# Four transformer layers in one program on one core: the opening in another order, and new slots in the plan of the attention items

## The chip, the cores and the metric

The kernel runs on one core of a Trainium2 chip, in one launch. What is measured is the device time in microseconds, the median over several executions. Lower is better.

## What is computed

The input is x, 4 batches of 512 rows of 128 features, with a context of 4 x 154 x 128 and masks over its 154 keys. Four layers follow one another. Each adds an attention over the context to x and then a feed-forward part:

```python
x = x + _L0_xattn_ref(_layernorm(x), ctx, ctx, mask_ik0, ...)   # 16 heads of 8, 64 memory keys and values beside the context's
x = x + _L0_ffn_ref(_layernorm(x), W1, b1, W2, b2, scale)        # gelu, low-rank terms taken from rows of the normalized x
x = x + _L1_xattn_ref(_layernorm(x), ctx, ...)                   # queries and keys scaled by their root mean square
x = x + _L1_ffn_ref(_layernorm(x), ...)                          # router, 4 experts of 512, silu
x = x + _L2_xattn_ref(_layernorm(x), ctx, ctx, mask_bf1, ...)    # rotary queries and keys
x = x + _L2_ffn_ref(_layernorm(x), ...)                          # router, 8 experts of 352 and a shared one of 176
x = x + _L3_xattn_ref(_layernorm(x), ctx, ctx, ...)              # one head of 128
x = x + _L3_ffn_ref(_layernorm(x), ...)                          # gate, two projections
```

## The kernel before

The work is cut into items: one part of one layer for one batch. Layers 0, 1 and 2 have four attention items each, numbered a = 0 to 11 here; the feed-forward items of layer 0 have no place of their own but are spread over the attention items 1 to 5, and the others (F1, F2, A3, F3) follow their layer's attention. Each engine runs its own instruction stream, written out by hand, and the streams meet at semaphores: an engine does its instructions strictly in the order of the code, and one that waits holds all behind it.

An attention item has 28 slots (layer 0, 7 chunks of keys by 4 groups of heads) or 20, and a tail of 3 or 4. In slot n TensorE computes one block of scores (`attention_step`, L1000, into bank 0 or 1), ScalarE its exponent (`exps`, L1773), and TensorE, some slots later, the products with the values (L1021) and with a mask for the denominators (L1031). The exponent's argument has the row's maximum already subtracted: the negated maxima are fed to the score matmul as rows of the queries' tile, and the head that each column belongs to is picked by constant rows of the keys' tile. So the item before must have prepared, for item a:

- keys: projection (`kproj`: `k_proj` L782, `k_bias` L1233), their square, mean square and Newton steps in layer 1 (`k1` to `k3`: L1890, L1239, L579 to L585), split in a high part and a low part (`ksplit` L1638 on ScalarE, `klow` L1930 on GpSimd), transposes (`kt`, L796), and copies into the keys' tile, one per head and masked, by ScalarE (`kb`, L1648) and VectorE (L1269);
- queries: the same on x (`xt` L843 and L1668, `q` L854 and L1289, `q1` to `q4`, `qsplit` L1690, `qlow` L1937), transposed per group (`qxt`, L865, copied at L1696);
- maxima: 32 score blocks over all keys for two heads each (`max`: `scores_for_max` L880), reduced by VectorE (`maxima`, L1327), transposed in two parts (`mt`, L890, L1703) and put into the queries' tile by DMAs (L629);
- values: `v`, L818, L820 and L1257.

The constant rows of the keys' tile, 5 partitions (96 to 100) of all columns, are written once per tile by `shift_rows` (L594) from the small table `maskk`: two tiles of layer 0 (`arena`, 3488 columns each) and two of the later layers (`kb_sb`, 2464 each). The 64 memory keys of layer 0 go into columns of both `arena` tiles (L1833, 4 heads each), after GpSimd scaled and split them (L2023 to L2030) and TensorE transposed them (L1171); the memory values are rows built at L2033.

Which slot of an item carries which piece is said by a table: a row of `SLOTS` serves two attention items (a // 2), a row of `SLOTS0` one batch of layer 0's feed-forward, whose slot numbers run on from attention item b + 1 into the next. `attention_plan` turns them into lists of pieces per slot, and each engine's loop takes the pieces that it has a part in. The pieces of a slot follow that slot's score block, exponent or values. `rden` are the reciprocals of the denominators (L1281, VectorE), `vs` the copy of the values (L1783, ScalarE), `on` their product (L1960, GpSimd), `finish` the output projection (L1043), `ln` and `norm` a layer norm (L1223, L1867 to L1884), `w` a chunk of feed-forward weights (DMA L645, ScalarE L1710, GpSimd L1966). `TAIL` is the number of slots that an item takes beyond its score blocks.

What precedes item 0 is the opening: constants and loads, then the preparation above for items 0 and 1, written out in each engine's code. PSUM has 8 banks; in the opening all are shared, in an attention item four (2 to 5) serve the preparation. `take_bank` picks the one taken longest ago, and TensorE waits until its last reader is done.

## Time and profile before

| | |
|---|---|
| median of 3 runs | 1012.13 us (1011.17 to 1013.39) |
| the profiled execution, own time | 1012.16 us |
| its span | 1010.4 us |
| TensorE's mean granted clock | 0.955 |
| busy: TensorE, VectorE, ScalarE, GpSimd | 912.1, 581.9, 432.4, 283.9 us |
| first score block of items 0, 1, 6, 8 | 58.55, 98.55, 332.28, 566.84 us |

PE is TensorE, DVE VectorE, ACT ScalarE, POOL GpSimd and SP the engine that issues the DMAs. The times of a timeline are microseconds from the span's start; the bracket tells how long the engine had been idle and what ended that. A releaser is inferred: of several semaphores it is the one that came last. The granted clock is 1.00 at 2.4 GHz and 0.50 at 1.2 GHz; a matmul is then twice as long. An fp32 matmul of this kernel counts as several instructions, so a group of 4 can be x8.

### The profile page before, as it was taken

What the parts mean: (1) busy time and instruction counts of PE and PEld (TensorE: products, weight loads), DVE (VectorE), ACT (ScalarE), POOL (GpSimd) and SP (SyncE); (2) the same over time, 40 slices, a digit from 0 to 9 for tenths busy, and PEclk for the clock granted to TensorE, in tenths of its full rate; (3) what the DMA queues carried; (4) which work ended last, traced back from release to release, by engine and by line L of the source; (5) the groups of instructions that cost most, each with busy time, mean ns of one, the idle gap of its engine ahead of it and who ended that gap; (6) DMA issues with size and microseconds to landing.
All of it is one profiled execution on the core that took longest, in us unless ns stands there. A gap on an engine that the chain in (4) does not pass through costs nothing. (4 is left out here: it accounts for less than half of the span.)

```text
span 1010.4 us, 15438 instructions
## 1 busy us (share of the span) xinstructions
PE 912.1 (90%) x5522; PEld 648.1 (64%) x5522; DVE 581.9 (58%) x1403; ACT 432.4 (43%) x795; POOL 283.9 (28%) x404
## 2 busy tenths in 40 slices
PE   2689999999999898999989799998999999999776
PEld 2555446465555444888877545545888878888665
DVE  3665757675757574455556367674536454354477
ACT  1345555667654555233332356655223232222330
POOL 7411514545644532010211055332001010010243
PEclk9989989999979799999999889999999999999995
DMA  6000000000010210000000211100000000000001
GB/s 153 4 2 14 1 15 2 15 2 18 19 53 2 76 36 9 14 1 1 1 1 1 77 29 37 44 24 13 2 1 1 1 1 1 1 1 1 1 1 42
DMA packets 27573, 18.10 MB, mean 18 GB/s; under 512 B 6221, under 2 KB 25770, under 8 KB 27370
## 3 DMA queue, kind: packets, MB, share of 16 engines
q1 hardware_dynamic: 27498, 17.12, 6.1%
q8 instruction: 45, 0.74, 0.3%
q14 instruction: 30, 0.25, 0.1%
HBM read 15.63 MB, written 1.05 MB: 17 GB/s over the span
## 5 line engine op out<-in xcount | busy, mean ns | idle before, releaser
L1327 DVE TENSOR_REDUCE mneg<-PS 128x2 f32<-128x308 f32 (+1 forms) x384 | 180.4, 515 | 115.5 <-PE PS L880 114.7
L1490 DVE TENSOR_TENSOR work<-PS,work 128x512 f32<-128x512 f32 (+2 forms) x168 | 114.8, 685 | 169.3 <-PE PS L1065 126.1
L1796 ACT ACTIVATE work<-PS 128x512 f32<-128x512 f32 (+2 forms) x168 | 99.8, 596 | 245.9 <-PE PS L1065 232.1
L1773 ACT ACTIVATE work<-PS 124x512 f32<-124x512 f32 (+1 forms) x272 | 156.8, 601 | 92.8 <-PE PS L1000 91.9
L1079 PEld LDWEIGHTS PS<-down_w,work 128*128 128x128 f32 (+2 forms) x1344 | 157.8, 191 | 5.7 <-DVE work L1490 1.3
L1079 PE MATMUL PS<-down_w,work 128*128 128x128 f32 (+2 forms) x1344 | 158.3, 275 | 1.0 <-DVE work L1490 1.0
L1063 PE MATMUL PS<-xh_sb,arena 128*128 128x512 f32 (+2 forms) x336 | 138.0, 411 | 9.6 <-DVE work L1490 9.6
L1065 PE MATMUL PS<-xh_sb,arena 128*128 128x512 f32 (+2 forms) x336 | 132.6, 395 | 0.0
L1064 PE MATMUL PS<-xl_sb,arena 128*128 128x512 f32 (+2 forms) x336 | 132.0, 393 | 0.0
L1867 POOL TENSOR_SCALAR rstd<-bn_mv 128x4 f32<-128x4 f32 x32 | 7.3, 227 | 436.2 <-DVE bn_mv L1225 436.1
L880 PEld LDWEIGHTS PS<-kb_sb,qxt_sb 97*128 97x128 f32 x256 | 45.4, 197 | 63.5 <-issue 33.8
L1000 PE MATMUL PS<-qxt_sb,kb_sb 101*124 101x512 f32 x160 | 71.3, 462 | 9.3 <-ACT work L1773 8.8
L1063 PEld LDWEIGHTS PS<-xh_sb,arena 128*128 128x128 f32 (+2 forms) x336 | 61.1, 182 | 28.8 <-DVE work L1490 14.3
L1021 PE MATMUL PS<-work,vb_sb 124*32 124x512 f32 (+1 forms) x544 | 78.2, 649 | 0.7 <-ACT work L1773 0.7
L880 PE MATMUL PS<-kb_sb,qxt_sb 97*128 97x308 f32 x256 | 71.7, 350 | 6.8 <-DVE mneg L1327 3.8
L1031 PE MATMUL PS<-work,mv_sb 124*32 124x512 f32 (+1 forms) x544 | 74.1, 618 | 0.0
L1065 PEld LDWEIGHTS PS<-xh_sb,arena 128*128 128x128 f32 (+2 forms) x336 | 60.9, 181 | 17.1
L1064 PEld LDWEIGHTS PS<-xl_sb,arena 128*128 128x128 f32 (+2 forms) x336 | 61.2, 182 | 12.6
L1518 DVE SCALAR_TENSOR_TENSOR x_res<-PS,gates_sb,x_res 128x128 f32<-128x128 f32 x192 | 53.5, 340 | 5.9 <-PE PS L1079 5.9
L1000 PE MATMUL PS<-qxt_sb,arena 101*125 101x512 f32 x112 | 50.8, 454 | 1.6 <-ACT work L1773 1.0
L880 PE MATMUL PS<-arena,qxt_sb 97*128 97x436 f32 x128 | 46.1, 416 | 6.0 <-DVE vb_sb L1257 2.8
L1000 PEld LDWEIGHTS PS<-qxt_sb,kb_sb 101*124 101x124 f32 x160 | 30.2, 195 | 29.9 <-ACT work L1773 21.9
(183 smaller groups left out, 1277.4 us busy)
## 6 DMA issues: line engine op xcount, KB each, us to landing
ctx_rep<-in_ctxT SPq DMA_DIRECT2D x12, 308.0 KB, 3.2
stage<-in_w SPq DMA_DIRECT2D x8, 256.0 KB, 4.2
stage<-in_wg SPq DMA_DIRECT2D x8, 176.0 KB, 2.4
stage<-in_wu SPq DMA_DIRECT2D x8, 176.0 KB, 2.4
x_res<-in_x SPq DMA_DIRECT2D x4, 256.0 KB, 3.9
down_w<-in_w SPq DMA_DIRECT2D x1, 1024.0 KB
...
```

What stands on the lines that cost most here:

```text
L880: pe.matmul(PS[:, bank, 0:w], QXT[0:KX_ROWS, a % 2, g, t * 128:(t + 1) * 128], KB(layer)[0:KX_ROWS, a % 2, g, f * w:(f + 1) * w], start=Tr ...
L1000: pe.matmul(PS[0:rows, n % 2, :], KB(layer)[0:K_ALL, a % 2, g, c * rows:(c + 1) * rows], QXT[0:K_ALL, a % 2, g, :], start=True, stop=True) ...
L1021: pe.matmul(PS[32 * g:32 * g + 32, 6, :], VB[0:rows, a % 2, c, g * 32:(g + 1) * 32], p_tile(i, 4 * c + g)[0:rows, :], start=(c == 0), stop ...
L1031: pe.matmul(PS[32 * g:32 * g + 32, 7, :], mask[0:rows, c, :], p_tile(i, 4 * c + g)[0:rows, :], start=(c == 0), stop=(c == chunks - 1)).the ...
L1063: pe.matmul(o, w[0], xH[:, i % 2, :], start=True, stop=False)
L1064: pe.matmul(o, w[0], xL[:, i % 2, :], start=False, stop=False)
L1065: pe.matmul(o, w[1], xH[:, i % 2, :], start=False, stop=True).then_inc(*sig["up"].mark((i, kt, m)))
L1079: mm = pe.matmul(PS[:, bank, t * 128:(t + 1) * 128], HH[0:rows, bank - 6, j, t * 128:(t + 1) * 128], rhs, start=(j == 0), stop=(j == len(t ...
L1327: dve.tensor_reduce(mneg[:, a % 2, t, h0:h0 + 2], PS[:, bank_of["mx", a, m], 0:2 * (KT0 if layer == 0 else KC)].rearrange("p (h n) -> p h ...
L1490: dve.tensor_tensor(HH[0:rows, e % 2, j, :], PS[0:rows, 2 * (n % 2) + 1, :], SS[0:rows, n % 2, :], ALU.mult).then_inc(*sig["h"].mark((i, n)))
L1773: act.activation(p_tile(i, n)[0:rows, :], PS[0:rows, n % 2, :], ACT.Exp, scale=SCALE).then_inc(*sig["p"].mark((i, n)))
L1796: act.activation(SS[0:rows, n % 2, :], PS[0:rows, bank, :], ACT.Silu).then_inc(*sig["act"].mark((i, n)))
```

## The change

1. `shift_rows` becomes an activation (Copy), and ScalarE does all four at the head of its stream, before the first x. The load of `maskk` goes to the head of SP's stream with a semaphore of its own.
2. VectorE: the masks' preparation comes ahead of item 0's key bias, the query bias ahead of the value bias; the layer norm sums of item 1 come ahead of `kb_out(0)`, and item 1's key and query biases stand after the 8th and the 14th maximum. The value masks move from after the 14th and 26th maximum to after the 20th and 26th.
3. TensorE: value bias after the queries' projection; the key transposes before those of the memory keys, which now wait for the memory keys alone (`"l"`) and not for the memory values; item 1's transposes and projections stand between the maxima. Bank 6 is held for the memory keys until the last of the opening's maxima.
4. ScalarE: the memory keys of item 0's tile are copied alone (4 operations), those of item 1's tile after its queries' split. `scores_for_max` waits for its own tile's.
5. GpSimd: item 0's low query part comes ahead of the memory keys, item 1's layer norm ahead of the memory values, and the two additions of the output bias to x are taken out of the layer norms and put behind item 1's low parts.
6. The table. Its rows for items 0 to 3 put `vs` and `rden` at slots 2 and 3 where there was 0 (item 0 has none). Queries, keys and weights move by one to four slots in all rows; of layer 0's feed-forward the last batch moves two slots forward, and all `ln` from 9 to 6. The tail of item 10 goes from 4 slots to 3.

```diff
-            eng.tensor_copy(KB(layer)[PR:K_ALL, r, :, 0:w].rearrange("p g (h n) -> p g h n", h=HL),
-                            maskk[PR:K_ALL, None, :, None].to_broadcast([K_ALL - PR, G, HL, w // HL])).then_inc(
+            eng.activation(KB(layer)[PR:K_ALL, r, :, 0:w].rearrange("p g (h n) -> p g h n", h=HL),
+                           maskk[PR:K_ALL, None, :, None].to_broadcast([K_ALL - PR, G, HL, w // HL]), ACT.Copy).then_inc(
...
+            load(maskk[:, :], A["maskk"], "maskk_in", 0)
             xv = A["x"].rearrange("b (t p) d -> p b t d", p=128)
...
                     if a < 2:
-                        pe.wait_ge(*sig["mem_kb"].at(0))
+                        pe.wait_ge(*sig["mem_kb"].at(a))
...
             k_proj(None, 0)
-            value_bias(None, 0)
             xt(None, 0)
             q_proj(None, 0)
-
-            pe.wait_ge(*sig["mem_ready"].at(0))
+            value_bias(None, 0)
+            k_transposes(None, 0)
+
+            pe.wait_ge(*sig["mem_ready"].at("l"))
...
-            k_transposes(None, 0)
-            xt(None, 1)
-            k_proj(None, 1)
             for g in range(G):
                 qxt(None, 0, g)
-            q_proj(None, 1)
             for m in range(N_MAX):
                 scores_for_max(None, 0, m)
-                if m == 8:
+                if m == 4:
+                    xt(None, 1)
+                    k_proj(None, 1)
+                if m == 10:
+                    q_proj(None, 1)
+                if m == 16:
                     v_blocks(None, 0, 0)
-                if m == 20:
+                if m == 22:
                     v_blocks(None, 0, 1)
...
+            act.wait_ge(*sig["maskk_in"].at(0))
+            for n in range(4):
+                shift_rows(act, n // 2, n % 2)
             xt_out(0)
...
-            layer_norm(0)
+            layer_norm(0, bias=False)
             k_finish(0)
             k_low(0)
+            q_low(0)
             pool.wait_ge(*sig["mem_in"].at(0))
...
+            layer_norm(1, bias=False)
             _, mem_cols = layout0(MR)
...
-            q_low(0)
-            layer_norm(1)
             k_finish(1)
             k_low(1)
             q_low(1)
-
-            pool.wait_ge(*sig["qx_l"].at(1))
-            for r_ in range(2):
-                shift_rows(pool, 1, r_)
-                pool.wait_ge(*sig["shift_rows"].at((True, r_)))
+            bias_into_x(0)
+            bias_into_x(1)
```

Of the table the row for items 8 and 9 stands here for all:

```diff
-    {"vs": 0, "rden": (0, 0, 0, 0), "on": 1, "finish": 6, "ln": (1, 2, 3, 4), "norm": 5, "kt": 0, "kb": (0, 0, 1, 1), "qxt": (2, 3, 5, 6),
-     "max": (5, 20), "mt": (1, 21), "v": (21, 20), "xt": 7, "q": 9, "q1": 11, "q2": 13, "q3": 14, "q4": 18, "qsplit": 19, "qlow": 20, "kproj": 13,
-     "k1": 10, "k2": 12, "k3": 14, "ksplit": 20, "klow": 21, "w": 4},
+    {"vs": 0, "rden": (0, 0, 0, 0), "on": 1, "finish": 6, "ln": (1, 2, 3, 4), "norm": 5, "kt": 0, "kb": (0, 0, 1, 1), "qxt": (3, 3, 5, 6),
+     "max": (5, 20), "mt": (1, 21), "v": (20, 21), "xt": 7, "q": 9, "q1": 11, "q2": 16, "q3": 16, "q4": 20, "qsplit": 21, "qlow": 22, "kproj": 12,
+     "k1": 10, "k2": 11, "k3": 14, "ksplit": 20, "klow": 21, "w": 7},
```

The order of ScalarE's instructions in the opening, before:

```order
L1668 ACT_TABLE_LOAD
L1668 ACTIVATE xt_sb<-PS 128x512
L1638 ACTIVATE kx_sb<-k_sb 77x8x4x8 x2
L1690 ACTIVATE qx_sb<-q_sb 128x16x4x8 x2
L1648 ACTIVATE arena<-PS,maskk_sb 97x2x154 x4
L1833 ACTIVATE arena<-PS,maskk_sb 97x4x64 x8
L1668 ACTIVATE xt_sb<-PS 128x512
L1696 ACTIVATE qxt_sb<-PS 97x512 x4
```

and with the change (its lines are numbered two higher there):

```order
L594 ACT_TABLE_LOAD
L594 ACTIVATE arena<-maskk_sb 5x4x872 x2
L594 ACTIVATE kb_sb<-maskk_sb 5x4x616 x2
L1670 ACTIVATE xt_sb<-PS 128x512
L1640 ACTIVATE kx_sb<-k_sb 77x8x4x8 x2
L1692 ACTIVATE qx_sb<-q_sb 128x16x4x8 x2
L1650 ACTIVATE arena<-PS,maskk_sb 97x2x154 x4
L1832 ACTIVATE arena<-PS,maskk_sb 97x4x64 x4
L1698 ACTIVATE qxt_sb<-PS 97x512 x4
```

The four constant rows stand ahead of all, half of the memory keys ahead of the query blocks, and item 1's x behind them. TensorE in the same place, before:

```order
L782 MATMUL PS<-w_attn,ctxT_sb 77x128 x2
L831 MATMUL PS<-w_attn,b_v 128x128
L843 MATMUL PS<-ident_sb,xn_sb 128x128 x4
L854 MATMUL PS<-w_attn,xt_sb 128x128 x4
L1171 MATMUL PS<-ident_sb,stage 97x64 x4
L796 MATMUL PS<-ident_sb,kx_sb 97x77 x8
L843 MATMUL PS<-ident_sb,xn_sb 128x128 x4
L782 MATMUL PS<-w_attn,ctxT_sb 77x128 x2
L865 MATMUL PS<-ident_sb,qx_sb 97x128 x16
L854 MATMUL PS<-w_attn,xt_sb 128x128 x4
L880 MATMUL PS<-arena,qxt_sb 128x436 x9
```

and with the change:

```order
L782 MATMUL PS<-w_attn,ctxT_sb 77x128 x2
L843 MATMUL PS<-ident_sb,xn_sb 128x128 x4
L854 MATMUL PS<-w_attn,xt_sb 128x128 x4
L831 MATMUL PS<-w_attn,b_v 128x128
L796 MATMUL PS<-ident_sb,kx_sb 97x77 x8
L1172 MATMUL PS<-ident_sb,stage 97x64 x4
L865 MATMUL PS<-ident_sb,qx_sb 97x128 x16
L880 MATMUL PS<-arena,qxt_sb 128x436 x5
L843 MATMUL PS<-ident_sb,xn_sb 128x128 x4
L782 MATMUL PS<-w_attn,ctxT_sb 77x128 x2
L880 MATMUL PS<-arena,qxt_sb 128x436 x6
L854 MATMUL PS<-w_attn,xt_sb 128x128 x4
```

Item 0's query blocks and first maxima no longer stand behind item 1's x. VectorE in item 5, where the queries and keys of item 7 are prepared (`mneg` are the maxima of item 6), before:

```order
L1327 TENSOR_REDUCE mneg<-PS 128x2 x15
L1289 TENSOR_TENSOR q_sb<-PS,b_q 128x512
L1233 TENSOR_TENSOR k_sb<-PS,b_k 77x256
L1327 TENSOR_REDUCE mneg<-PS 128x2 x4
L1239 TENSOR_REDUCE k_ms_sb<-ka_sb 77x32
L571 TENSOR_SCALAR k_ms_sb<-k_ms_sb 77x32
L573 TENSOR_SCALAR k_rr_sb<-k_ms_sb 77x32
L1327 TENSOR_REDUCE mneg<-PS 128x2 x2
L1297 TENSOR_REDUCE q_ms_sb<-qa_sb 128x64
L571 TENSOR_SCALAR q_ms_sb<-q_ms_sb 128x64
L573 TENSOR_SCALAR q_rr_sb<-q_ms_sb 128x64
L1327 TENSOR_REDUCE mneg<-PS 128x2 x8
```

and with the change:

```order
L1331 TENSOR_REDUCE mneg<-PS 128x2 x14
L1293 TENSOR_TENSOR q_sb<-PS,b_q 128x512
L1237 TENSOR_TENSOR k_sb<-PS,b_k 77x256
L1331 TENSOR_REDUCE mneg<-PS 128x2 x3
L1301 TENSOR_REDUCE q_ms_sb<-qa_sb 128x64
L571 TENSOR_SCALAR q_ms_sb<-q_ms_sb 128x64
L573 TENSOR_SCALAR q_rr_sb<-q_ms_sb 128x64
L1243 TENSOR_REDUCE k_ms_sb<-ka_sb 77x32
L571 TENSOR_SCALAR k_ms_sb<-k_ms_sb 77x32
L573 TENSOR_SCALAR k_rr_sb<-k_ms_sb 77x32
L1331 TENSOR_REDUCE mneg<-PS 128x2 x6
```

Two maxima come ahead of these rows in both. The queries' seed (L573, `q_rr_sb`) now comes first, after 19 of the item's 32 maxima instead of 23, and the keys' follows it.

## Rows read from the trace of the kernel before

**Rows 1.** The page: busy us (share of the span) xinstructions of each engine.

```profile
PE 912.1 (90%) x5522; PEld 648.1 (64%) x5522; DVE 581.9 (58%) x1403; ACT 432.4 (43%) x795; POOL 283.9 (28%) x404
```

**Rows 2.** Timeline, 10-24 us: start, us, engine, line, operation [idle before <-releaser].

```profile
11.93 0.60 ACT L1668 ACTIVATE xt_sb<-PS 128x512 f32<-128x512 f32 x1 [9.93 <-PE PS L843]
...
12.58 2.07 PE L854 MATMUL PS<-w_attn,xt_sb 128*128 128x128 f32 x8 [0.69 <-ACT xt_sb L1668]
...
13.33 4.28 DVE L594 CAST arena<-maskk_sb 5x3488 fp32r<-5x3488 f32 x2
...
13.45 2.33 POOL L1920 TENSOR_TENSOR k_sb<-k_sb,keep 77x256 f32<-77x256 f32 x1 [0.66 <-DVE kbias L1590]
...
17.64 0.69 DVE L1289 TENSOR_TENSOR q_sb<-PS,b_q 128x512 f32<-128x512 f32 x1
...
18.32 0.55 POOL L2023 TENSOR_SCALAR stage<-stage 64x128 f32<-64x128 f32 x1
...
18.37 1.15 ACT L1690 ACTIVATE qx_sb<-q_sb 128x512 fp32r<-128x512 f32 x2 [1.84 <-DVE q_sb L1289]
...
19.54 0.45 POOL L2030 TENSOR_TENSOR stage<-stage 64x128 f32<-64x128 f32 x1
...
22.46 0.91 PE L1171 MATMUL PS<-ident_sb,stage 64*97 64x64 f32 x4 [7.80 <-POOL down_w L2033]
...
22.48 1.26 POOL L1937 TENSOR_TENSOR qx_sb<-q_sb,qx_sb 128x512 f32<-128x512 f32 x1
```

**Rows 3.** The timeline, 24 to 59 us.

```profile
26.54 3.04 ACT L1833 ACTIVATE arena<-PS,maskk_sb 97x256 fp32r<-97x256 f32 x8
...
31.72 1.11 PE L843 MATMUL PS<-ident_sb,xn_sb 128*128 128x128 f32 x4 [6.83 <-POOL xn_sb L1874]
...
33.48 3.21 PE L865 MATMUL PS<-ident_sb,qx_sb 128*97 128x128 f32 x16
...
34.23 0.61 POOL L1920 TENSOR_TENSOR k_sb<-k_sb,keep 77x256 f32<-77x256 f32 x1 [1.15 <-DVE k_sb L1233]
...
37.34 2.07 PE L880 MATMUL PS<-arena,qxt_sb 97*128 97x436 f32 x9
...
53.76 3.23 DVE L1327 TENSOR_REDUCE mneg<-PS 128x2 f32<-128x436 f32 x6
...
58.55 0.79 PE L1000 MATMUL PS<-qxt_sb,arena 101*125 101x512 f32 x1 [0.49 <-DMA qxt_sb<-mt_sb]
```

**Rows 4.** Groups by form, ScalarE: busy us, mean ns | idle before.

```profile
L1796 ACT ACTIVATE work<-PS 128x512 f32<-128x512 f32 x128 | 76.1, 597 | 149.4 <-PE PS L1065 135.6 <-PE PS L1043 12.1 <-DVE work L1490 1.5
...
L1821 ACT ACTIVATE work<-PS 77x1024 f32<-77x1024 f32 x4 | 4.1, 1019 | 4.2 <-PE PS L1136 4.2
```

**Rows 5.** DMA issues of the first 60 us: KB, us to landing.

```profile
bqk_sb<-in_bk SPq DMA_DIRECT2D x1, 0.5 KB, 2.1
```

**Rows 6.** Timeline, end of item 5 and start of 6: GpSimd, then TensorE.

```profile
324.07 0.29 POOL L579 TENSOR_TENSOR q_tmp<-q_rr_sb 128x64 f32<-128x64 f32 x1 [3.34 <-DVE q_rr_sb L573]
...
335.63 0.72 POOL L1930 TENSOR_TENSOR kx_sb<-k_sb,kx_sb 77x256 f32<-77x256 f32 x1
...
336.41 1.53 PE L796 MATMUL PS<-ident_sb,kx_sb 77*97 77x77 f32 x8 [3.64 <-POOL kx_sb L1930]
```

**Rows 7.** The timeline in item 8: ScalarE, then TensorE.

```profile
579.65 0.50 ACT L1710 ACTIVATE arena<-stage 128x352 fp32r<-128x352 f32 x1 [4.89 <-DMA stage<-in_wg]
...
581.17 0.55 PE L880 MATMUL PS<-kb_sb,qxt_sb 97*128 97x308 f32 x2 [1.98 <-ACT qxt_sb L1696]
```

**Rows 8.** The timeline at the start of item 1: VectorE.

```profile
98.77 3.39 DVE L1281 RECIPROCAL work<-PS 128x128 f32<-128x128 f32 x4 [0.55 <-PE PS L1031]
```

**Rows 9.** Windows, L1000 alone: us, busy (instructions), PEclk, DMA share, GB/s.

```profile
336.50:346.80 10.30, 4.15 (x6) 1.75 (x6) 0.50 0.14 53
...
346.80:357.10 10.30, 3.18 (x8) 1.48 (x8) 1.00 0.01 2
...
582.30:589.10 6.80, 1.41 (x2) 0.65 (x2) 0.50 0.11 30
```

More of the change, by code:

```diff
@@ L673, in _ @@
                     load(mvT[:, :], A["mvT0"], "mem_in", 0)
-                    load(maskk[:, :], A["maskk"], "const_in", 0)
                     load(MV0[:, :, :], A["mv0"], "const_in", 0)
@@ L1821, in attention3_step, with memory_keys @@
                     act.activation(PT3, PS[0:KJ, 6:8, :], ACT.Copy).then_inc(*sig["a3_pt"].mark(i))
+            def memory_keys(r):
+                if r == 0:
+                    act.wait_ge(*sig["mem_kt_psum"].at(0))
+                act.wait_ge(*shift_signal(0).at((False, r)))
+                mem_cols = KB0[:, r, :, 0:HL * KT0].rearrange("p g (h n) -> p g h n", h=HL)[:, :, :, KC:KT0]
+                for h in range(HL):
+                    act.activation(mem_cols[0:KX_ROWS, :, h, :], PS[0:KX_ROWS, 6, 0:G * KM].rearrange("p (g n) -> p g n", g=G), ACT.Copy,
+                                   scale=maskk[0:KX_ROWS, h:h + 1]).then_inc(*sig["mem_kb"].more(r))
+            act.wait_ge(*sig["maskk_in"].at(0))
+            for n in range(4):
+                shift_rows(act, n // 2, n % 2)
             xt_out(0)
@@ L1827, in _ @@
                 kb_out(0, h)
-            act.wait_ge(*sig["mem_kt_psum"].at(0))
-            for r_ in range(2):
-                mem_cols = KB0[:, r_, :, 0:HL * KT0].rearrange("p g (h n) -> p g h n", h=HL)[:, :, :, KC:KT0]
-                for h in range(HL):
-                    act.activation(mem_cols[0:KX_ROWS, :, h, :], PS[0:KX_ROWS, 6, 0:G * KM].rearrange("p (g n) -> p g n", g=G), ACT.Copy,
-                                   scale=maskk[0:KX_ROWS, h:h + 1]).then_inc(*sig["mem_kb"].more(0))
-            xt_out(1)
+            memory_keys(0)
             for g in range(G):
                 qxt_out(None, 0, g)
+            xt_out(1)
             k_split(1)
             q_split(1)
+            memory_keys(1)
             mt_out(None, 0, 0)
@@ L1857, in _, with layer_norm @@
         def _(pool):
-            def layer_norm(j):
+            def layer_norm(j, bias=True):
                 b = ITEMS[j][2]
@@ L1875, in layer_norm, with bias_into_x @@
                                    ALU.mult).then_inc(*sig["xn"].mark(j))
-                slot = bias_slot(j)
+                if bias:
+                    bias_into_x(j)
+            def bias_into_x(j):
+                b, slot = ITEMS[j][2], bias_slot(j)
                 if slot is not None:
```

25 lines of the change are left out of this document (13 added, 12 removed), and 44 rows, old and new, of tables (SLOTS, SLOTS0).

## Prediction

> **What bounds the kernel now.** The page's busy shares come first: TensorE is busy for 90% of the span, VectorE 58%, ScalarE 43%, GpSimd 28% [rows 1]. So time is to be had only where TensorE is idle, or where its clock is at the half level; the page's clock line shows such slices in the opening, in the attention items and at the end. The timeline of the opening comes next, because there TensorE is busy for little of the time: the first exponent's score matmul starts at 58.55 us [rows 3]. Two chains fill that time. The first is GpSimd's: it works one thing after the other, and TensorE, in order, stands 7.80 us for the memory keys' and values' preparation, although the keys alone (L2023 to L2030, done at 19.99) are what its next transposes read [rows 2]. Then it waits 6.83 us for the second item's normalized x at 31.72, with the queries of item 0, whose low part GpSimd had finished at 23.74, queued behind it [rows 2, 3]. The second chain is VectorE's: 32 maxima that TensorE feeds from 37.34 and that end at 56.99, 0.53 us each (the last six took 3.23), with two value masks between them [rows 3]. The last view is the timeline at TensorE's stalls in the attention items, with the windows for the clock there.
>
> **The opening.** I follow the changed order along the chain.
>
> Constant rows. VectorE did two casts of 3488 columns in 4.28 us from 13.33 [rows 2], GpSimd two of 2464 after 40.9. All four go to ScalarE. No row has such an operation there; the nearest are 1024 columns in 1.019 us and 512 in 0.597 [rows 4], so 0.824 ns a column: 0.597 + 2976 x 0.824 ns = 3.05 us for 3488 columns and 2.21 us for 2464, 10.5 us for the four; neighbours overlap by a tenth of a microsecond, so 10.2. The Trainium skill speaks against the move (ScalarE: Activation LUTs, Rules for kernel authors: plain arithmetic belongs on VectorE, which is faster by the column). The rows agree on the column, 2.14 against 3.05 us, and by that rule alone the change would lose 0.9 us on each of the two large casts, 1014 us; rival 2 is its strong form. What decides is not the column's price, but that ScalarE has nothing to do until 11.93 [rows 2]. The selector table's load becomes SP's first: small loads land 2.1 us after issue [rows 5], so from 0.72 us, with a microsecond of doubt for the first of all, it is there at 2.8 to 3.8, and ScalarE is free at about 13.4. Every other load is issued 0.3 to 0.45 us later. The transposed x is copied from 13.5 where it would have been 12.2: **ScalarE's queue costs 1.3 us** here (0 if the columns ran as on VectorE, 4 if they were twice as dear).
>
> Queries of item 0. Copy until 14.1; the projection, 2.07 us at 1.2 GHz [rows 2], until 16.2; bias 0.69, no longer behind the casts, until 17.0; split 1.15: 18.2; GpSimd's low part 1.26: 19.5 [rows 2]. On GpSimd the key multiplication took 2.33 us beside the casts and 0.61 without [rows 2, 3], so the keys' low part is done by about 15.7, and the key transposes and their copies fall between 17 and 20.3, beside the queries' chain. Memory keys: four small operations, 18.32 to 19.99 before, so 1.7 us, until 21.2. Their transposes 0.91: 22.1 [rows 2]. Then sixteen query transposes, 3.21 us [rows 3], until 25.3, while ScalarE copies half of the memory keys (eight took 3.04 [rows 3], so 1.5) and the first query block by 24.4. **The maxima begin on TensorE at about 25.3 instead of 37.34: 12.0 us earlier.** For the rest of the opening the price goes up: one key bias (some 0.4, half as wide as the query's) and one query bias (0.69 [rows 2]) now stand between the maxima. 12.0 - 1.1 = **10.9 us earlier** at their end (46.1). The transposes of the maxima, their DMA and the first score follow as before. What is moved behind is covered: normalizing item 1 on GpSimd 21.2 to 24.8, the value rows (the 2.5 us between 19.99 and 22.46 [rows 2]) until 27.3, wanted by the 17th maximum's matmul at about 33; item 1's keys and queries by 37; two bias additions of 512 columns, as long as the low part (1.26), until 40; the second half of the memory keys 1.5 us after that split. All this is ahead of 46; without it, it would hold item 1's first slots. Bounds: 7 us (twice the price for ScalarE's columns, and another microsecond of bank waits, since bank 6 is withheld from the maxima) to 13.
>
> **The table.** Items are numbered 0 to 11 by attention item.
> - Item 6 starts with TensorE idle for 3.64 us, for item 7's low keys, which GpSimd makes at 335.63 after 24 Newton steps that began at 324.07, when VectorE delivered the seed [rows 6]. The seed now stands after 19 of the item's maxima where it stood after 23, two slots of some 1.5 us earlier. GpSimd works the rest through without a pause, so it ends 3.0 us earlier. What is late next is the score before it. Behind that stall lies a stretch at 0.50 of the clock with 6 score matmuls in 10.3 us, and 8 in the next 10.3 at 1.00 [rows 9]: two slots, 2.6 us. Half the stall's clock loss may come back: I take **-5.0** (bounds 0 and -6.2).
> - Item 8: ScalarE waits 4.89 us for the first weight chunk, queued before the exponents of slots 4 and on, and TensorE then 1.98 us [rows 7]; 6.8 us at 0.50 follow [rows 9]. With the chunk at slot 7 three exponents go first, 3 x about 1 us; the landing at 579.6 doesn't move, since SP issues it behind the 17 loads of the down weights. **-3.0** (stall, and a part of the clock by the ratio above, 0.25 x 6.8 = 1.7; bounds 0 and -3.7).
> - Items 1 to 3: VectorE's four reciprocals, 3.39 us [rows 8], go from ahead of the keys' copy to slot 3. The second key bank comes free 3.4 us sooner, and TensorE's short waits for it go; the first maxima then meet the reciprocals instead. **-1.0** for the three (bounds -4 and +5).
> - The other moves by a slot or two, the tail of item 10, and the later weight chunks of items 9 to 11 (the last at slot 20 of 24, some 2 us before its use) **0** (+-3).
>
> **Sum.** The profiled execution took 1012.16 us, beside a median of 1012.13. 1012.2 - 10.9 - 5.0 - 3.0 - 1.0 = 992.3; I say **992**.
>
> **Rivals.**
> 1. The table gives nothing (20%). VectorE, GpSimd and ScalarE do the same work, and a stall that is taken from one slot turns up in another: item 5's query finish now stands 3 slots behind a seed whose Newton steps take 4.5 us, and VectorE would stand for it with maxima behind it. For it: TensorE is 90% busy, and idle time is spread in pieces under 1 us. Against it: the 3.64 and 1.98 us have a cause each that the edit touches. The opening alone: 1012.2 - 10.9 = 1001, +-3.
> 2. ScalarE's rows become the opening's bound (8%). If 5 partitions of broadcast columns cost twice the slope, ScalarE is free at 23.6, not 13.4, and the whole chain behind it is 10 us late: it would eat the 10.9 us but for the table's 9: about 1002. Against it: the same 5 partitions gave VectorE no trouble (2.14 us for 3488 columns, 0.61 ns each [rows 2]), and the copies on ScalarE, of 77 and 128 partitions, leave a start cost of 0.18 us by one slope [rows 4].
> 3. Slower (4%). The reciprocals at slot 3 hold VectorE for 3.39 us [rows 8] just as the first maxima arrive. TensorE has four banks for them and for the query transposes; if it fills them it stands for 3.4 us, and the clock falls as it does behind item 6's stall, which cost 2.6 us [rows 9]: 6.0 us an item, in items 1, 2 and 3, 18.0. The late chains of items 3 and 4 then take the gains of items 6 and 8 along, which hang on when those chains start: 1012.2 - 10.9 + 18.0 = 1019. It decides from 3.6 us an item on (3 x 3.6 = 10.9), and from 6.3 on if items 6 and 8 keep their 8.0. For it: the first maxima are VectorE's, and TensorE can't pass them. Against: before, the same 3.39 us stood just ahead of the first maximum, so that VectorE reaches it no later than it did.
> 4. More than forecast (8%): further half-clock stretches, of which the page's clock line shows several between 100 and 300 us, go with the moves in items 1 and 4. Four of them at 2 us, item 8's clock part and a little: another 8 us, about 984.
>
> **The numbers.** The forecast's own case holds 60%, 986 to 998. 983 to 1003 takes in most of it and of rivals 1 and 2. A measurement of this kernel tells 0.2%, 2 us, from no change. Faster by more: 60 + 20 + 8 + 8 = 96, less 2 for rivals 1 and 2 where they come out worse than their middle: 94%. Within: 2%. Slower: 4%.
>
> **What would show it.** ScalarE: four activations of 5 partitions from about 3 us, 3.05 and 2.2 us each. First L880 on TensorE at 25.3, last maximum at 46, first score at 47.6. No TensorE wait over 1 us at the start of item 6; no ScalarE wait for a weight chunk over 2 us in item 8. It is wrong if the first score comes later than 52 us, or if from there to the end the kernel takes more than 953.6 us, as it does now (1012.16 - 58.55).

## The result, and the profile after

The changed kernel takes 975.72 us in the median (974.32 to 976.58), the kernel before 1012.76 beside it: a ratio of 0.9632, 95% interval 0.9605 to 0.9659. It is 37 us faster, 16 more than the forecast's 992, and lies outside the range given.

The page of the changed kernel, busy time by engine, beside [rows 1]: TensorE is busy for 17 us less, though its work is the same.

```profile
span 973.1 us, 15438 instructions
PE 895.2 (92%) x5522; PEld 638.0 (66%) x5522; DVE 574.7 (59%) x1401; ACT 443.9 (46%) x799; POOL 275.9 (28%) x402
```

Its timeline in the opening, beside [rows 2, 3]:

```profile
2.65 6.11 ACT L594 ACTIVATE arena<-maskk_sb 5x3488 fp32r<-5x3488 f32 x2 [0.65 <-DMA maskk_sb<-in_maskk]
...
7.42 1.04 POOL L1882 TENSOR_TENSOR xn_sb<-x_res,bn_mv 128x512 f32<-128x512 f32 x1
...
8.66 4.38 ACT L594 ACTIVATE kb_sb<-maskk_sb 5x2464 fp32r<-5x2464 f32 x2
...
13.06 0.60 ACT L1670 ACTIVATE xt_sb<-PS 128x512 f32<-128x512 f32 x1
...
17.77 1.27 POOL L1953 TENSOR_TENSOR qx_sb<-q_sb,qx_sb 128x512 f32<-128x512 f32 x1 [2.57 <-ACT qx_sb L1692]
...
20.23 0.45 POOL L2047 TENSOR_TENSOR stage<-stage 64x128 f32<-64x128 f32 x1
...
20.73 0.91 PE L1172 MATMUL PS<-ident_sb,stage 64*97 64x64 f32 x4 [3.25 <-POOL stage L2047]
...
24.96 1.44 PE L880 MATMUL PS<-arena,qxt_sb 97*128 97x436 f32 x3
...
45.57 0.60 PE L890 MATMUL PS<-ident_sb,mneg 128*4 128x128 f32 x4 [2.04 <-DVE mneg L1331]
...
45.92 0.47 PE L1000 MATMUL PS<-qxt_sb,arena 101*125 101x512 f32 x1
```

The four constant rows end at 13.04, the first maxima matmul starts at 24.96 and the first score at 45.92, where it was 58.55 [rows 3]. The opening gives 12.6 us. The other 24.7 come behind it: 23.6 in the attention items, 1.1 in the last layers. The windows view, one stretch an item (from its first score to the next item's), of the kernel before, items 1 to 4, 6, 8 and 10; columns are the stretch, its length, busy time of PE, PEld, DVE, ACT and POOL, the granted clock, DMA share and GB/s:

```profile
98.60:151.90 53.30, 49.61 (x280) 26.00 (x277) 33.33 (x63) 30.05 (x53) 15.47 (x17) 0.90 0.03 8
151.90:202.00 50.10, 47.92 (x311) 27.92 (x307) 34.60 (x70) 29.31 (x53) 25.48 (x44) 1.00 0.03 8
202.00:250.80 48.80, 46.58 (x303) 26.95 (x299) 31.25 (x71) 32.09 (x56) 25.47 (x44) 0.97 0.01 2
250.80:295.40 44.60, 41.28 (x244) 24.61 (x243) 30.84 (x70) 24.32 (x46) 26.49 (x45) 0.89 0.13 35
332.30:369.10 36.80, 32.43 (x191) 18.29 (x187) 21.45 (x49) 18.62 (x37) 14.62 (x21) 0.86 0.15 53
566.80:606.70 39.90, 34.66 (x193) 18.36 (x191) 20.47 (x52) 20.43 (x40) 14.48 (x18) 0.83 0.23 66
636.80:669.10 32.30, 30.29 (x193) 16.02 (x192) 21.68 (x49) 17.80 (x35) 8.39 (x9) 0.95 0.09 25
```

The same items of the changed kernel:

```profile
85.10:132.80 47.70, 46.69 (x281) 25.37 (x277) 31.05 (x62) 29.86 (x53) 15.46 (x17) 0.96 0.04 9
132.80:183.70 50.90, 49.12 (x311) 28.51 (x307) 34.90 (x70) 29.87 (x53) 25.50 (x44) 0.97 0.03 8
183.70:233.80 50.10, 48.21 (x301) 26.99 (x298) 31.21 (x71) 32.48 (x56) 25.67 (x44) 0.93 0.01 2
233.80:273.90 40.10, 38.26 (x254) 23.47 (x252) 30.70 (x71) 24.97 (x46) 25.68 (x45) 1.00 0.08 25
309.10:342.70 33.60, 31.21 (x191) 17.10 (x187) 21.27 (x49) 18.07 (x35) 12.17 (x16) 0.90 0.17 58
540.50:574.00 33.50, 29.97 (x194) 16.60 (x192) 21.15 (x52) 20.11 (x40) 13.23 (x17) 0.95 0.24 69
604.10:633.10 29.00, 27.17 (x186) 14.76 (x184) 20.87 (x48) 18.48 (x38) 11.06 (x12) 1.00 0.14 38
```

Read two things in each row: length less PE busy is TensorE's idle time (item 1: 3.7, then 1.0 us); and twice the length times (1 - clock) is the time at the 1.2 GHz level, in which the same matmuls keep PE busy for longer (item 1: 10.2, then 3.4 us, by the clock before it is rounded). Over items 0 to 11, with TensorE's waits of more than 0.1 us added up from the timeline:

| | items 0 to 11 | idle | at half clock |
|---|---|---|---|
| before | 448.3 us | 31.6 | 56.1 |
| changed | 424.8 | 20.0 | 27.3 |

### The profile page after: what moved, and what is told of

It reads as the page before. It is cut to its first block and busy times, and to the rows that moved or that the text cites. A ratio compares the mean times of both kernels' runs of the same rounds, so it can differ in the third digit from the quotient of the medians.

```text
span 973.1 us, 15438 instructions
## 1 busy us (share of the span) xinstructions
PE 895.2 (92%) x5522; PEld 638.0 (66%) x5522; DVE 574.7 (59%) x1401; ACT 443.9 (46%) x799; POOL 275.9 (28%) x402
## 5 line engine op out<-in xcount | busy, mean ns | idle before, releaser
L1063 PEld LDWEIGHTS PS<-xh_sb,arena 128*128 128x128 f32 (+2 forms) x336 | 61.0, 182 | 28.8 <-DVE work L1494 14.2
L1000 PE MATMUL PS<-qxt_sb,kb_sb 101*124 101x512 f32 x160 | 68.9, 448 | 9.0 <-ACT work L1775 8.7
L1021 PE MATMUL PS<-work,vb_sb 124*32 124x512 f32 (+1 forms) x544 | 75.3, 626 | 0.7 <-ACT work L1775 0.7
L1064 PEld LDWEIGHTS PS<-xl_sb,arena 128*128 128x128 f32 (+2 forms) x336 | 61.2, 182 | 12.6
L1000 PE MATMUL PS<-qxt_sb,arena 101*125 101x512 f32 x112 | 50.1, 447 | 0.2 <-ACT work L1775 0.2
L1000 PEld LDWEIGHTS PS<-qxt_sb,kb_sb 101*124 101x124 f32 x160 | 29.1, 189 | 28.8 <-ACT work L1775 19.2
```

The lines of the kernel that those rows point to most:

```text
L1000: pe.matmul(PS[0:rows, n % 2, :], KB(layer)[0:K_ALL, a % 2, g, c * rows:(c + 1) * rows], QXT[0:K_ALL, a % 2, g, :], start=True, stop=True) ...
L1021: pe.matmul(PS[32 * g:32 * g + 32, 6, :], VB[0:rows, a % 2, c, g * 32:(g + 1) * 32], p_tile(i, 4 * c + g)[0:rows, :], start=(c == 0), stop ...
L1063: pe.matmul(o, w[0], xH[:, i % 2, :], start=True, stop=False)
L1064: pe.matmul(o, w[0], xL[:, i % 2, :], start=False, stop=False)
```

## The experiments

Fifteen kernels ran. Ratios are to the kernel before in the same session, with their 95% intervals; "idle" and "half" are TensorE's waits and its time at half clock in items 0 to 11, in us, in the one run of each kernel that was profiled. The difference of two ratios has an interval of some 3 to 7 us either way; it is given where a reading hangs on it.

| kernel | median us | ratio | first score | idle | half |
|---|---|---|---|---|---|
| changed | 975.72 | 0.9632 (0.9605-0.9659) | 45.92 | 20.0 | 27.3 |
| e1 | 1000.43 | 0.9873 (0.9818-0.9928) | 45.92 | 30.7 | 54.4 |
| e2 | 989.90 | 0.9761 (0.9722-0.9800) | 59.74 | 19.5 | 32.5 |
| e3 | 987.63 | 0.9735 (0.9692-0.9777) | 45.86 | 24.5 | 54.5 |
| e4 | 988.81 | 0.9746 (0.9709-0.9784) | 46.44 | 23.0 | 45.9 |
| e5 | 992.60 | 0.9789 (0.9752-0.9826) | 45.94 | 23.9 | 51.2 |
| e6 | 993.17 | 0.9805 (0.9758-0.9852) | 45.95 | 29.3 | 40.8 |
| e7 | 974.63 | 0.9615 (0.9584-0.9646) | 43.45 | 19.9 | 34.1 |
| e8 | 979.28 | 0.9660 (0.9625-0.9695) | 46.91 | 20.1 | 34.1 |
| e9 | 991.41 | 0.9789 (0.9773-0.9806) | 46.05 | 27.4 | 44.4 |
| e10 | 981.89 | 0.9713 (0.9668-0.9758) | 46.01 | 21.3 | 34.1 |
| e11 | 987.26 | 0.9729 (0.9696-0.9762) | 45.94 | 21.6 | 43.7 |
| e12 | 973.67 | 0.9607 (0.9593-0.9622) | 43.01 | 19.9 | 34.1 |
| e13 | 995.95 | 0.9819 (0.9785-0.9854) | 46.48 | 28.6 | 56.1 |
| e14 | 983.38 | 0.9695 (0.9656-0.9733) | 46.12 | 21.6 | 41.0 |
| e15 | 977.73 | 0.9666 (0.9624-0.9708) | 44.13 | 20.3 | 32.3 |

**e1 and e2: opening alone, tables alone.** Edits: the changed kernel with `SLOTS`, `SLOTS0` and `TAIL` of before; the kernel before with the new ones.

> The changed kernel's opening with the three tables of before. Theory A (the two halves of the change add up, each gains in its own place): the first exponent's score starts 12.6 us earlier, at 45.9 us, and from there to the end takes what it took before, so 1012.8 - 12.6 = 1000 us, and the last item's end stays 12.6 us ahead to within 2 us. Theory B (the half-clock stretches fall where the chains happen to stand, so that the same table after another opening meets other stretches): the time lies more than 3 us from 1000, and the difference in start times between items wanders by 3 us or more from item to item. The forecast on record had 1001.

> The kernel before with the three tables of the change. Theory A (additive): 1012.8 - (37.0 - 12.6) = 988.4 us, with the item-by-item gains of the changed kernel behind its first score: 5.7 us in item 1, some 5 in item 4, 3 to 4 in items 6 and 10, 6.5 in item 8. Theory B (the gains depend on the phase that the new opening gives): less than two thirds of 24.4 us, so above 996 us. The forecast on record had 9 us for the tables, 1003.

Theory A holds for the two halves: 0.9873 x 0.9761 = 0.9637, beside 0.9632 for both. The opening is worth 13 us (e1's interval: 7 to 18), the tables 24 (20 to 28). Inside e1 the items do wander, by 2.9 us between their starts: item 1 takes 1.6 us less than before and item 6 2.8 less, item 3 1.6 more, each with 3.4 or 6.8 us less or more at half clock. Item 6 is the one to note, since its stall is there in full:

```profile
324.90 1.01 PE L780 MATMUL PS<-ident_sb,kx_sb 77*97 77x77 f32 x8 [3.64 <-POOL kx_sb L1930]
```

It takes 34.0 us in e1 all the same, where it took 36.8, because 3.4 us of it are at half clock and not 10.2. In e2, with the new table, it takes 30.1.

**e3 and e4: the table by halves.**

```
e3: SLOTS rows 0, 1 and all of SLOTS0 as before
e4: SLOTS rows 2 to 5 and TAIL as before
```

> The changed kernel with rows 0 and 1 of SLOTS and all of SLOTS0 as before (items 0 to 3, and what SLOTS0[3] puts into items 4 and 5). Theory A: it loses what items 1 to 3 gave, 4.3 us (start of item 4: 16.9 us ahead instead of 12.6), and, if the stall in item 4 went because of SLOTS0[3] and not because of SLOTS row 2, the 4.6 us of item 4 too: 980 us in the first case, 984.6 in the second. Theory B: items 6, 8 and 10 change their gain too, by 2 us or more.

> The changed kernel with rows 2 to 5 of SLOTS and TAIL as before (items 4 to 11). Theory A: it keeps the 16.9 us at the start of item 4 and loses the rest, 19.2 us: 995 us; 990 if the 4.6 us of item 4 hang on SLOTS0[3], which stays new. Item 6 starts with TensorE idle for 3.6 us again, and item 8 with 2.0. Theory B: item 6's stall and the half-clock stretch behind it differ from before's, by over 2 us.

The early part is worth 0.0103 of the time, 10.4 us (interval 5 to 16), where 4.3 or 8.9 were expected, and the late part 11.5 (7 to 16), where 19.2 or 14.3 were. So the first case of each is a miss, and the second, which gives item 4's 4.6 us to `SLOTS0[3]`, is within the noise. Together the halves give 21.9 of the tables' 24. The single items do not follow, though. Item 4 takes 43.5 us in e3 and 43.1 in e4, 3 us more than in the changed kernel in both, and in e3 item 1 takes 54.7 us, more than it did before the change. Items 1 and 4 of e3:

```profile
86.50:141.20 54.70, 51.16 (x281) 26.79 (x277) 33.34 (x63) 29.93 (x53) 15.47 (x17) 0.88 0.03 7
240.20:283.70 43.50, 41.64 (x245) 24.71 (x243) 28.33 (x70) 24.61 (x46) 26.22 (x45) 0.88 0.13 37
```

Item 4 is idle for 1.8 us here, as in the changed kernel, with no wait over 0.7 us; but it has 10.2 us at half clock, where the changed kernel has none.

**e5 and e6: four moves.**

```
- "vs": 0, "rden": (0, 0, 0, 0)           rows 0, 1
+ "vs": 2, "rden": (3, 3, 3, 3)
- "kproj": 13, "k2": 12, "klow": 20       row 3
+ "kproj": 12, "k2": 11, "klow": 18
- "w": 4   - "w": 5                       rows 4, 5
+ "w": 7   + "w": 8
  SLOTS0[3] as in the change
e5: these four alone, in e1.   e6: these four back, in the changed kernel.
```

> The changed kernel's opening with the tables of before, in which four moves alone are made: the reciprocals and value split of items 1 to 3 (vs 2, rden 3), SLOTS0[3] as in the change (item 4), row 3's key steps (items 6 and 7: kproj 12, k2 11, klow 18), and the weight chunks of items 8 to 11 (w 7 and 8). Theory C (a few moves carry the table, each by the stall that it takes away): items 1, 4, 6 and 8 take what they take in the changed kernel (47.6, 40.1, 33.5, 33.4 us), and the time is 1000 - 19 = 981 us. Theory D (the many small moves of the query and key steps, costed at nothing in the forecast, carry it): 992 us or more, with items 1 and 4 above 51 and 43 us.

> The changed kernel with the same four moves taken back. Theory C: it loses what the four gave: 975.7 + 19 = 995 us. Theory D: 983 us or less, items 1 and 4 near their 47.6 and 40.1 us. Either way the sum of the gains of this kernel and the last one against the opening alone tells whether the moves add up (24.4 us).

Neither C nor D. The time of e5 and its items 1 and 4 (54.2 and 45.1 us) are as theory D has them; e6 has theory C's time with theory D's items (48.2 and 40.9). Alone the four give 8.5 us, all the rest alone 6.9, and together they give 24.4. So 9 us of the gain belong to no part alone; the interval of that number is 0.3 to 18 us. Idle time adds up in part: 6.8 and 1.4 us alone, 10.7 together. Half-clock time adds up less: 3.2 and 13.6 alone, 27.1 together.

It led to a reckoning in place of prices by move. Over the 12 items of 17 traces (the kernel before, the changed one and these fifteen), an item takes its own fixed time plus 0.94 of its idle time plus 0.43 of its half-clock time, by least squares, with a scatter of 0.36 us. (The expectations from e9 on use 0.97 and 0.43, from fewer traces.) By it the 23.6 us gained in the items are 0.94 x 11.6 = 10.9 of idle time and 0.43 x 28.8 = 12.4 of clock. It says where the time of an item goes; it does not say what makes the clock fall.

**e7: memory keys first on GpSimd.** Edit: the four operations on the memory keys (`mk`) ahead of `k_low(0)` and `q_low(0)`.

> The changed kernel with GpSimd's preparation of the memory keys (1.7 us) put ahead of the low parts of item 0's keys and queries, into the time in which GpSimd waits (2.05 and 2.57 us idle). Theory A (the opening's chain now runs through GpSimd: queries' low part at 19.0, then memory keys until 20.7, then TensorE's transposes): TensorE's transposes of the memory keys move from 20.7 to before 19.0, the query transposes start at about 19.3 instead of 21.6, first score at 43.9 instead of 45.9, time 973.7 us. Theory E (something else follows within a microsecond: the key transposes, VectorE's copy of the second key half at 18.2, or the 32 maxima on VectorE): first score at 45 or later, time within 1 us of 975.7.

The timeline of e7: the transposes of the memory keys and of the queries.

```profile
17.42 0.91 PE L1172 MATMUL PS<-ident_sb,stage 64*97 64x64 f32 x4
...
19.10 3.73 PE L865 MATMUL PS<-ident_sb,qx_sb 128*97 128x128 f32 x16 [0.77 <-POOL qx_sb L1953]
```

The chain is as theory A has it: first score at 43.45, 2.5 us earlier. By the ratios, 0.9615 beside 0.9632, the whole gains 1.7 us, give or take 4, which neither shows nor refutes the 2.0 expected. The two profiled runs have the same span, 973.1 us: the same table with the same idle time met 34.1 us of half clock in place of 27.3, and 0.43 x 6.8 = 2.9 us ate the gain there.

**e8: two constant rows on VectorE.** Edit: `shift_rows(dve, 0, r_)` as casts ahead of `k_bias(0)`; ScalarE keeps layer 1's.

> The changed kernel with the constant rows of layer 0 (two of 3488 columns) by VectorE as casts, between its mask work and the key bias, where it is idle for 4.0 us; ScalarE keeps the two of 2464 columns. Theory F (the forecast's term: ScalarE's queue costs the opening about 1 us): the transposed x is copied at 12.0 instead of 13.1, the first score comes 1 us earlier, 974.7 us. Theory G (the casts and GpSimd's work on x hold each other up, as they did before the change, where GpSimd's key multiplication took 2.33 us beside the casts and takes 0.61 now): one of GpSimd's 1.04 us operations between 6.3 and 9.6 takes over 2 us, the first score comes 1 to 3 us later, 977 to 979 us.

```profile
7.22 4.71 DVE L596 CAST arena<-maskk_sb 5x3488 fp32r<-5x3488 f32 x2
7.44 2.65 POOL L1886 TENSOR_TENSOR xn_sb<-x_res,bn_mv 128x512 f32<-128x512 f32 x1
...
10.17 2.65 POOL L1889 TENSOR_TENSOR xn_sb<-xn_sb,rstd 128x512 f32<-128x512 f32 x1
```

Theory G, in the trace. Beside VectorE's casts GpSimd's two operations take 2.65 us each where they take 1.04, x is ready later, and the first score comes 1.0 us later although ScalarE is free 6 us sooner. (The whole is slower by 0.0028, 3 us, give or take 4.5: not clear of noise.) The Trainium skill (SBUF — State Buffer, section "SBUF: two separate sides") says that GpSimd and certain operations of VectorE, those in a two-port mode or with two inputs in SBUF, share a pair of ports, which whichever starts first holds to its end while the other waits; the trace agrees with a hold-up, of 1.6 us a time.

**e9, e10, e11: the table by kinds of step**, each taking something else back in items 1 to 3, 4 to 7 and 8 to 11.

```
e9:  q..qlow of rows 0, 1 and SLOTS0[0..2]; all of SLOTS0[3]; w of rows 4, 5
e10: vs, rden of rows 0, 1; kproj..klow of rows 2, 3; q..qlow, qxt of rows 4, 5
e11: ln 9 in SLOTS0[0..2]; q..qlow, qxt, kb, w of rows 2, 3; kproj..klow of rows 4, 5; TAIL
```

> The changed kernel with three things back as before: the query steps of items 1 to 3 (rows 0 and 1, and SLOTS0[0] to [2]), all of SLOTS0[3], and the weight chunks of items 8 to 11 (w 4 and 5). Theory H (an item takes its fixed work, plus 0.97 of TensorE's idle time in it, plus 0.43 of its time at the half clock; idle time goes with the moves one by one, half-clock time does not): the wait of 1.6 us behind VectorE's 2.87 us x_low operation returns in item 1 (idle 2.6 us instead of 0.96), item 4's idle time rises from 1.8 to 2.4 and item 8's from 3.5 to about 6.5, together 5.2 us idle, so at least 981 us; the half-clock time of items 0 to 11 rises too, and each item fits the formula to 1 us. Theory C (each of these moves takes its own stall and its own clock stretch): item 1 takes 53, item 4 44 and item 8 39.5 us, others as in the changed kernel: 991 us.

> The changed kernel with three other things back: reciprocals and value split of items 1 to 3 (vs 0, rden 0), the key steps of rows 2 and 3 (items 4 to 7), and the query steps of rows 4 and 5 (items 8 to 11). Theory H: item 1's idle time rises from 0.96 to 1.9 us, item 6's from 2.4 to 3.7; item 8 keeps its 3.5 to within 1 us, since the weight chunks stay late. Some 2.5 to 4 us idle, 978 to 980 us before what the half clock adds. Against it: item 8 above 36 us, which would say that the late weight chunks need the later query steps beside them.

> The changed kernel with the moves back that the forecast costed at nothing and no run has tried alone: the statistics at slot 9 instead of 6 (SLOTS0[0] to [2]), the query steps, qxt, kb and w of rows 2 and 3 (items 4 to 7), the key steps of rows 4 and 5, and TAIL. Forecast: nothing, 976 us +-1. Theory H: idle time of items 1 to 11 changes by less than 2 us, and what the time changes beyond that is half-clock time at 0.43 us each. Theory D (the small moves carry what the four did not, some 7 us): 980 us or more.

Three things come out. First, in e9 item 8 has its weight chunk ahead of the exponents again. ScalarE and TensorE there (lines stand 16 lower in kernels with another table):

```profile
560.22 0.50 ACT L1696 ACTIVATE arena<-stage 128x352 fp32r<-128x352 f32 x1 [4.54 <-DMA stage<-in_wg]
...
561.75 0.70 PE L864 MATMUL PS<-kb_sb,qxt_sb 97*128 97x308 f32 x2 [3.84 <-ACT qxt_sb L1682]
```

It is the wait of [rows 7], longer by 1.9 us on TensorE, and item 8 takes 38.3 us. The idle time of all items rises by 7.4 us, not 5.2, because item 6's stall is back too. Second, item 1's wait does not return in e9, against the expectation, though it does in part in e11, where for item 1 `ln` alone is back: x_low, VectorE's subtraction that makes the low part of x (`xl_sb`), takes 2.30 us there, where it takes 0.68 to 0.84 in every kernel with `ln` 6, and item 1 takes 50.9 us instead of 47.6. Third, the moves that the forecast costed at nothing, as e11 takes them back, are worth 9.8 us by the ratios (interval 5.5 to 14), with 1.6 of idle time and 16.4 of half clock. That is 1.5 and 7.1 us by the reckoning, so theories H and D both come. e10 is a miss in part: item 1 idles 1.9 us and item 8 3.0, as expected, but item 6 idles 2.1, not 3.7, and in all the idle time rises by 1.3 us, not 2.5 to 4. One of its four runs took 991.55 us, at a mean clock of 0.960, and the others 981.7 to 982.0 at 0.970: the half clock moves between runs of one kernel too.

**e12: ScalarE's two rows for layer 1 later, on top of e7.** Edit: `range(4)` to `range(2)`, and `shift_rows` for layer 1 behind `memory_keys(1)`.

> The kernel with the memory keys first (e7), and besides ScalarE's two constant rows of 2464 columns moved behind item 1's query split; the two of 3488 stay first. It tests the forecast's term that ScalarE's queue costs the opening 1.3 us. If it does, the transposed x is copied at 12.1 instead of 13.07 (TensorE's transposes end about 12.0), and the first score starts 0.9 us before e7's 43.45, at 42.5. If not, at 43.4. As for the whole: by theory H the items' idle time stays 19.9 us, and the time is 974.6 - 0.9 = 973.7 us, give or take 3 us for half-clock stretches that move.

```profile
12.61 0.60 ACT L1670 ACTIVATE xt_sb<-PS 128x512 f32<-128x512 f32 x1 [3.85 <-PE PS L843]
```

x is now copied as soon as TensorE has transposed it, 0.46 us earlier than in e7, and the first score comes 0.44 earlier, not 0.9: in that run the key projection began at 10.61, in e7's at 10.33, so it transposed x from 11.51 on, where e7 did from 11.23. ScalarE's queue cost about 1.1 us in the changed kernel (transposed at 12.0, copied at 13.06), beside 1.3 forecast. This is the fastest median, 0.9607. Its interval (0.9593 to 0.9622) and the changed kernel's just overlap, so it isn't shown to be faster.

**e13: `ln` 6 in place of 9, and the tail, alone.**

> The changed kernel's opening with the tables of before, and two of their numbers new: ln 6 instead of 9 in SLOTS0[0] to [2] (items 1 to 3), and item 10's tail 3 instead of 4. In the runs so far VectorE's x_low operation of item 1 takes 2.87 us wherever ln is 9 with the old query steps, 2.30 with the new ones, and 0.69 to 0.84 with ln 6. Theory L (the slot of the statistics alone decides whether x_low lies beside GpSimd's work): x_low takes under 0.9 us, item 1's idle time falls from 3.66 to about 2.1 us and its half-clock time by 3.4 us or more, item 1 takes 49 us instead of 51.8. The tail: item 10 takes 1.2 us less, item 11 about as much more or less. Time 997 to 998 us beside 1000 for the opening alone. Against it: x_low over 2 us, time 1000.

The timeline around x_low in item 1, of the kernel before:

```profile
125.14 1.30 POOL L1978 TENSOR_TENSOR lora_diag<-lora_rows,eye_sb 4x512 f32<-4x512 f32 x1
126.06 2.87 DVE L1336 TENSOR_TENSOR xl_sb<-xt_sb,xh_sb 128x512 fp32r<-128x512 f32 x1
126.41 0.60 POOL L1920 TENSOR_TENSOR k_sb<-k_sb,keep 77x256 f32<-77x256 f32 x1
...
127.11 1.26 POOL L1937 TENSOR_TENSOR qx_sb<-q_sb,qx_sb 128x512 f32<-128x512 f32 x1
...
129.51 0.46 PE L880 MATMUL PS<-arena,qxt_sb 97*128 97x436 f32 x1 [1.62 <-DVE mneg L1327]
```

and of e13:

```profile
110.88 0.60 POOL L1920 TENSOR_TENSOR k_sb<-k_sb,keep 77x256 f32<-77x256 f32 x1
...
113.96 0.68 DVE L1324 TENSOR_TENSOR xl_sb<-xt_sb,xh_sb 128x512 fp32r<-128x512 f32 x1
114.01 1.77 POOL L1937 TENSOR_TENSOR qx_sb<-q_sb,qx_sb 128x512 f32<-128x512 f32 x1 [2.39 <-ACT qx_sb L1676]
```

Theory L: one number of the table takes x_low out from between GpSimd's operations. Before, x_low ended 0.56 us after the last of the three. Now it starts just ahead of the queries' low part and takes 0.68 us, not 2.87 (2.85 in e1), while GpSimd's operation takes 1.77 and not 1.26. The wait of 1.62 us is gone, and item 1 takes 48.1 us where the opening alone left 51.8. It is the same sharing as in e8, the other way round. Item 10 takes 2.8 us less, 1.5 of it clock and 1.2 the shorter tail. The ratio falls by 0.0054, 5.5 us, more than the 2 to 3 expected, but give or take 7, so the whole time shows nothing here; and items 6 and 7 had 13.6 us more at half clock in the profiled run than in e1's.

**e14: useless work.** Edit: x_low of item 1 and the last query bias, in item 9, four times over.

> The changed kernel with useless work on VectorE in two places: x_low of item 1 done four times over (three more of 0.69 us), and the last query bias, in item 9, four times over (three more of 0.67 us). It asks what idle time of TensorE does to the clock with nothing else moved. Theory H (idle time brings half-clock time with it): TensorE's idle time rises by 1 to 2 us in item 1 and in item 9 by 0 to 2, and the half-clock time of the item or of the next by 3.4 us or more for each stall over 1 us: 975.7 + 2.5 + 0.43 x 6.8 = 981 us. Theory P (the half-clock stretches are a matter of where the items lie, not of the stalls): the idle time is all that is paid, 978 us.

Its windows for items 1, 9 and 10:

```profile
86.80:138.20 51.40, 49.07 (x280) 25.48 (x276) 32.87 (x65) 30.00 (x53) 15.43 (x17) 0.93 0.03 8
582.00:614.80 32.80, 31.10 (x198) 17.47 (x198) 24.50 (x55) 19.29 (x40) 16.85 (x20) 0.95 0.10 27
614.80:645.30 30.50, 28.75 (x180) 15.94 (x180) 21.06 (x49) 18.43 (x38) 8.46 (x10) 0.94 0.13 38
```

The idle time rises by 1.25 us in item 1 and 0.9 in item 9, and each of items 1, 9 and 10 has 3.4 us more at half clock; they take 3.8, 2.6 and 1.5 us more. The ratio rises by 0.0063, 6.4 us (interval 2 to 11) for 1.6 us more idle time; all four runs, 981.1 to 984.6 us, lie above theory P's 978. Theory H, with a reserve. Items 0, 4, 5 and 8, which no edit touched, also had 3.4 us more at half clock each, and items 3 and 6 had 3.4 and 6.8 less. The better comparison is e7, whose table is the same too: it has e14's half-clock time in every item but two, and item 9's 3.4 us are among it, without the edit. Beside e7, e14 has 3.4 us more in item 1 and 3.4 in item 10, and nothing else. So the wait in item 1 seems to have brought a stretch in its own item, and the one in item 9 perhaps the stretch in the next; that rests on one profiled run of each.

**e15: a version put together from idle times.** Edit: e12 with rows 2 and 3's key steps and row 4's query steps as before.

> A version drawn from the items' idle times: e12 with the key steps of rows 2 and 3 as before (items 4 to 7 were idle 6.4 us instead of 7.4) and the query steps of row 4 as before (item 8 idle 2.9 instead of 3.2 to 3.5). By theory H: idle time of the items 18.5 to 19 us instead of 19.9, so 972.5 us beside 973.7 for e12, give or take 3 us for the half clock. Against it: 974 us or more, which would say that idle time below 20 us is not what sets the time any more.

A miss: 0.9666, 6 us (give or take 5) above e12, which it was to beat. Items 4 and 8 were less idle (0.7 and 2.4 us), but item 10, whose queries row 4 prepares, 3.3 instead of 1.8, and the items' sum was 20.3 us, not 18.5 to 19. Four runs took 975.4 to 978.6 us at a mean clock of 0.971 to 0.973, the other two 985.4 and 986.9 at 0.960, as one run of e10 did.

## Why the prediction was off

The signs that the forecast named came: the four activations, the times of the opening within 2 us, no wait over 1 us at the start of item 6, no wait of ScalarE for a weight chunk in item 8. What was off is the price of the table: 24.7 us came behind the first score where 9.0 were forecast.

**The opening, -10.9: right in its chain, 1.7 us short.** ScalarE's four activations took 6.11 and 4.38 us for each pair, 10.4 with what lies between, forecast 10.2; x was copied at 13.06 (13.5), the query transposes started at 21.57 (22.1), the maxima at 24.96 (25.3) and ended at 45.5 (46.1). From there to the first score the forecast kept 1.5 us. It took 0.4, since the clock no longer stood at 0.50 there and the DMA of the maxima was no longer waited for [rows 3]. The weighing of the rows' place missed its best reason: on VectorE they would bring the first score 1.0 us later (e8), not for their columns but for GpSimd's work beside them. The forecast's bound of 7 us contradicts its own rival 2: it has ScalarE's columns cost the chain 4 us if they are twice as dear, where rival 2 rightly adds some 10. As they cost 3.1 us for 3488 columns, this was not put to the test.

**Item 6, -5.0: measured -3.3, and that number is in part chance.** The mechanism of the stall is right. GpSimd's Newton steps began 11.1 us ahead of item 6 where it had been 8.2, so 2.85 us earlier (forecast 3.0), and the stall went from 3.64 us [rows 6] to 0.82:

```profile
298.08 0.29 POOL L579 TENSOR_TENSOR q_tmp<-q_rr_sb 128x64 f32<-128x64 f32 x1 [1.69 <-DVE q_rr_sb L573]
...
310.46 0.91 PE L796 MATMUL PS<-ident_sb,kx_sb 77*97 77x77 f32 x8 [0.82 <-POOL kx_sb L1946]
```

It is `SLOTS0[3]` that does it. In every kernel with that row old (before, e1, e3, e6, e9, e13) the stall is 3.16 to 3.64 us, in all others it is under 0.9; e9, with row 3's key steps new, has it at 3.17, and e10, with them the other way, at 0.82. Of the 10.2 us at half clock in the item 3.4 went. But e1 lost 6.8 of them with the stall in place and took 34.0 us, and e7, e12 and e14, with the changed kernel's table, have none and take 30.1. What the stall itself is worth is its idle time, 2.0 us over the item.

**Item 8, -3.0: measured -6.5.** The stall of 1.98 us [rows 7] is gone, but the idle time fell only by 1.7; 4.4 us are the clock, 13.7 us at half down to 3.4, for which the forecast had at most 1.7 us. Two sizes were off: its ratio of 0.25, where the runs give 0.43, and the stretch, 6.8 us, where 10.2 went.

**Items 1 to 3, -1.0: measured -3.5,** 5.7 less in item 1, 0.8 and 1.4 more in items 2 and 3, each with 3.4 us more at half clock. The reciprocals at slot 3 gave some 1 us of idle time (e5: 3.66 to 2.60 in item 1). The rest in item 1 is `ln` (e13), which stood among the moves at nothing.

**The other moves, 0 (+-3): measured -11.4. This is the step that failed.** Item 4 gave 4.6 us, item 10 3.4, item 5 1.6, item 0 0.8, the last layers 1.1. By the reckoning the items among these had 4.5 us less idle time, worth 4.2, and 15 us less at half clock, worth 6.5; and item 10's shorter tail, also at nothing, gave 1.2 (e13). e11, which takes such moves back, loses 9.8 us with 16.4 us of half clock. The forecast's sentence took moves by a slot or two as moves of work on engines with time to spare. It left out two things. Such a move can put operations of VectorE and GpSimd side by side or take them apart; this is shown in item 1. And the time at half clock was priced only behind two stalls that had been picked out, when more than half of the items' gain is clock.

How far each of the two goes outside item 1 is not shown. One can add up by how much VectorE's and GpSimd's operations in items 0 to 11 exceed their usual length (the tenth percentile of the same operation over the 17 traces). Before it is 14.2 and 7.2 us, in the changed kernel 14.5 and 6.8: item 1 lost 2.1 us of it on VectorE, items 7 to 9 gained 2.6. So fewer collisions are not what the table as a whole gave. And why item 4 lost its 10.2 us at half clock stays open: e3 has them all at the same idle time.

Rival 4 named further half-clock stretches in items 1 and 4, which is what came, but gave them 8 us and 8 in 100. Rivals 1 to 3 did not come: the reciprocals met the first maxima without a wait of note. The part that came as forecast, the opening, was reasoned along one chain of waits. The part that did not is a sum over twelve items, and its clock differs even between kernels with one table (e7).
